# Moving GpSimd's routing-weight multiply ahead of VectorE's gating in a fused attention and mixture-of-experts kernel

## The reference

```
q, k = exp(x Wq' + bq), exp(x Wk' + bk);  v = x Wv' + bv          # 16 heads of 8
attn = causal linear attention: sum_s<=t (q_t . k_s) v_s / sum_s<=t (q_t . k_s)
x1   = layernorm(x + attn Wo' + bo)
w    = routing weights of 32 experts: sigmoid scores, best 2 of 4 expert groups,
       best 8 experts in these, normalised and scaled by 2.5; 0 for the others
y    = shared(x1) + sum_e w[t, e] * down_e( silu(gate_e x1) * (up_e x1) )
out  = layernorm(x1 + y)
```

## Time and profile before

| | us |
|---|---|
| median of 3 runs (lowest to highest) | 462.87 (462.61 to 464.24) |
| profiled execution | 463.29 |
| its span, first to last instruction | 461.5 |
| PE / PEld busy | 424.0 / 324.8 |
| DVE busy | 347.4 |
| POOL busy | 282.4 |
| ACT busy | 273.3 |

### The profile page before, as it was taken

The page is one execution under the profiler, slowest core; times in us unless marked ns, Lnnn a source line. Parts: engine busy times, 40 slices in busy tenths (PEclk is TensorE's granted clock), DMA queues, the critical chain, the costliest instruction groups (busy, mean ns, idle before and its releaser), DMA issues.

```text
span 461.5 us, 10791 instructions
## 1 busy us (share of the span) xinstructions
PE 424.0 (92%) x3954; PEld 324.8 (70%) x3954; DVE 347.4 (75%) x909; ACT 273.3 (59%) x530; POOL 282.4 (61%) x208
## 2 busy tenths in 40 slices
PE   5855799999999999999999999999999999899982
PEld 3733587778867787778877787778877787578761
DVE  2678548797878968797878968796878968777652
ACT  3835334963587546963587546963587546555642
POOL 2565236864676557864677557764677557757781
PEclk9989589999999999999999999999999999999996
DMA  7400544346440823446340923446440913466500
GB/s 233 187 1 1 147 92 90 92 97 141 93 113 7 197 69 82 91 103 135 91 116 12 202 68 74 90 104 134 91 116 9 200 41 81 91 134 129 121 11 23
DMA packets 28660, 45.08 MB, mean 98 GB/s; under 512 B 1984, under 2 KB 10304, under 8 KB 28224
## 3 DMA queue, kind: packets, MB, share of 16 engines
q1 hardware_dynamic: 28608, 44.40, 41.2%
HBM read 41.77 MB, written 2.62 MB: 96 GB/s over the span
## 4 chain that ended last, share of the span: by engine, by line
PE 40%; DVE 32%; issue 12%; POOL 8%; ACT 2%; DVEq 1%; ACTq 0%; POOLq 0%
PE bank L326 39%; DVE units L866 7%; POOL units L958 5%; DVE stats L741 2%; DVE hidden_lo L721 2%; POOL rstd L977 2%; DVE top_of_group L782 2%; DVE x L753 2%; DVE bank L775 1%; ACT hidden_hi L584 1%; DVE replaced L814 1%; DVE out_sb L878 1%; DVE k_sum L847 1%; DVE probs L731 1%; DVE kv_blocks L836 1%
## 5 line engine op out<-in xcount | busy, mean ns | idle before, releaser
L958 POOL TENSOR_TENSOR units<-units,weight_wide 128x512 f32<-128x512 f32 x128 | 174.3, 1367 | 130.5 <-DVE units L866 115.9
L602 ACT ACTIVATE units<-bank 128x512 f32<-128x512 f32 x136 | 80.7, 594 | 79.2 <-PE bank L326 78.9
L866 DVE TENSOR_TENSOR units<-bank,units 128x512 f32<-128x512 f32 x136 | 92.9, 683 | 35.1 <-PE bank L326 28.0
L584 ACT ACTIVATE hidden_hi<-units 128x512 fp32r<-128x512 f32 x136 | 86.1, 634 | 53.7 <-POOL units L958 47.7
L721 DVE TENSOR_TENSOR hidden_lo<-units,hidden_hi 128x512 fp32r<-128x512 f32 x112 | 97.7, 873 | 19.6 <-ACT hidden_hi L584 18.8
L326 PE MATMUL bank<-x_hi,gate_hi 128*128 128x512 f32 x136 | 62.1, 457 | 2.0 <-DVE units L866 1.6
L326 PE MATMUL bank<-hidden_hi,down_hi 128*128 128x512 f32 x136 | 55.0, 404 | 1.7 <-DVE hidden_lo L721 1.7
L326 PE MATMUL bank<-x_hi,up_hi 128*128 128x512 f32 x136 | 54.7, 403 | 1.8 <-ACT units L602 1.8
L326 PE MATMUL bank<-x_lo,gate_hi 128*128 128x512 f32 x136 | 54.6, 401 | 0.0
L326 PE MATMUL bank<-x_hi,gate_lo 128*128 128x512 f32 x136 | 54.4, 400 | 0.0
L326 PE MATMUL bank<-x_hi,up_lo 128*128 128x512 f32 x136 | 54.1, 398 | 0.0
(11 more groups left out here) (107 smaller groups left out, 670.8 us busy)
## 6 DMA issues: line engine op xcount, KB each, us to landing
weight_wide<-weight_d SPq DMA_DIRECT2D x62, 512.0 KB, 6.7
xT<-xT_in SPq DMA_DIRECT2D x8, 256.0 KB, 6.8
x_tok<-x_in SPq DMA_DIRECT2D x8, 256.0 KB, 6.9
out_dram<-out_sb SPq DMA_DIRECT2D x8, 256.0 KB, 2.3
weight_wide<-up_in SPq DMA_DIRECT2D x1, 1088.0 KB, 9.0
up_raw<-up_in SPq DMA_DIRECT2D x1, 1088.0 KB, 11.0
down_raw<-down_in SPq DMA_DIRECT2D x1, 1088.0 KB, 13.2
weight_d<-weightT SPq DMA_DIRECT2D x8, 64.0 KB, 1.6
```

The source lines that it names most:

```text
L584: nc.scalar.activation(hidden_hi[place(n, g)][:, :], units[place(n, g)][:, :], ACT.Copy).then_inc(hidden_hi_done, 1)
L602: nc.scalar.activation(units[place(n, g)][:, :], up_banks[2 * n % 3][:, :], ACT.Silu).then_inc(silu_done, 1)
L866: V.tensor_tensor(units[place(n, g)][:, :], up_banks[(2 * n + 1) % 3][:, :], units[place(n, g)][:, :], ALU.mult).then_inc(gated_done, 1)
L958: G.tensor_tensor(units[place(n, g)][:, :], units[place(n, g)][:, :], weight_wide[:, (n - 1) % (2 * PIECE), :], ALU.mult).then_inc(hidden_ ...
```

## The change

In groups 1 to 7 steps 3 and 4 change places for the routed blocks: POOL multiplies the silu's result by the weight as soon as the silu is done, and DVE's gating takes that product. The high part then waits for the gating. Block 0, which has no weight, and the whole of group 0 keep their order. No instruction is added or taken away, and none changes its place in its own queue; only what three of them wait for is another.

```
 high_part (ACT)
-                if n == 0:
-                    act.wait_ge(gated_done, reached(BLOCKS * g + 1))
+                if n == 0 or g > 0:
+                    act.wait_ge(gated_done, reached(BLOCKS * g + n + 1))
                 else:
-                    act.wait_ge(hidden_done, reached(ROUTED * g + n))
+                    act.wait_ge(hidden_done, n)
 slot (DVE), ahead of the gating
                     dve.wait_ge(u_ready, reached(BLOCKS * g + n + 1))
-                    dve.wait_ge(silu_done, reached(BLOCKS * g + n + 1))
+                    if g == 0 or n == 0:
+                        dve.wait_ge(silu_done, reached(BLOCKS * g + n + 1))
+                    else:
+                        dve.wait_ge(hidden_done, ROUTED * g + n)
 slot (POOL), ahead of the multiply
-                    pool.wait_ge(gated_done, reached(BLOCKS * g + n + 1))
+                    if g == 0:
+                        pool.wait_ge(gated_done, n + 1)
+                    else:
+                        pool.wait_ge(silu_done, BLOCKS * g + n + 1)
```

## The result

| | us |
|---|---|
| before, median of 4 runs (lowest to highest) | 463.21 (462.61 to 464.24) |
| after, median of 4 runs | 503.29 (501.93 to 505.33) |
| ratio, with its 95% interval | 1.087 (1.085 to 1.090) |
| profiled execution after, and its span | 502.46, 500.7 |

The changed kernel is 40.1 us slower; 497 was forecast, from 480 to 510. The lines of the changed kernel are a little lower in the file: the gating is L869, the multiply L964, the powers L973 and L983, attnT L893, x_lo L988, k_sum L950.

The account below looks back on a forecast made before the run. PE was taken to set the pace, busy 51.15 of a steady group's 51.7 us. Groups 1 to 5 add 27.5, group 6 5.0, group 7 2.0, together 34.5, giving 497 us, range 480 to 510.

Parts of the forecast that it names:

- First stall: Multiply 5 stands behind rstd2 on POOL, so gating 5 and attnT are late; PE's projection weight load slips 2.77 us.
- Second stall: Multiply 7 stands behind rstd1 on POOL, so gating 7 and block 9's gate matmul are late; +5.05 us in all.
- Given back and lost again: Later slots: router's exponential slips only 4.3 us (-0.75); then multiply 10 behind x_lo and 16 behind k_sum; +5.5 per group.
- Low parts: DVE's low part 4 is held up beside a POOL multiply, 1.57 us against a mean of 0.87.
- the walk: Step-by-step forecast through group 3 using the rows' own durations, giving +5.5 us per steady group.
- rival 2: Low parts meet running POOL multiplies more often on DVE's tight stretch: 4 us a group, 24 in all, 521; chance 0.09.
- Sum: Groups 1 to 5 add 27.5 us, group 6 5.0, group 7 2.0, group 0 nothing: 34.5 in all.
- only the first stall stays: The shorter chain behind the gating and freed DVE waits absorb all but the projection stall: +19, 482 us; chance 0.12.
- faster: Multiply hides between silu and up matmuls in slots 8 to 16 and the end: 457 us; chance 0.05.
- no effect: The gating is late only where PE has cover: 463 us; chance 0.04.
- port collisions: Some six low parts a group held 0.70 us beside POOL's multiply, on top of the forecast: 521 us; chance 0.09.
- Rival 1: Only the projection stall stays; the shorter chain behind the gating absorbs the rest: 482 us; chance 0.12.

Follow-up runs that it names:

- experiment 2: Kernel before, with gating and multiply changing places only in blocks 5 and 7 of groups 1 to 7; 487.22 us, ratio 1.051.
- experiment 5: Changed kernel with POOL's rstd2 and shift2 moved behind the multiply of block 6 and rstd1 behind that of block 7; 481.50 us, ratio 1.040.
- experiment 4: Changed kernel with rstd2 behind multiply 5, rstd1 behind multiply 7, x_lo behind multiply 10, POOL's low parts one slot later; 485.90 us, ratio 1.048.
- kernel 6: As experiment 5, but in groups 1 to 6 only blocks 1 to 9 have gating and multiply exchanged; 474.28 us, ratio 1.024.
- experiment 1: Changed kernel with POOL's rstd2 moved behind the multiply of block 5 and rstd1 behind that of block 7; 486.52 us, ratio 1.049.
- experiment 7: Changed kernel with no rstd or shift on POOL: power left out, DVE writes variance plus eps and makes shift2; 470.88 us, ratio 1.019.
- experiment 8: Kernel before with no rstd or shift on POOL: power left out, DVE writes variance plus eps and makes shift2; 454.20 us, ratio 0.981.

## Why the prediction was right

Point by point, in the order of its steps (times of after less 10.32):

- *First stall.* attnT at PE: forecast 228.10, measured 228.17; PE's wait forecast 2.77, measured 2.83. Experiments 2 and 5 confirm the cause.
- *Second stall.* The gate matmul of block 9: forecast 235.6, measured 235.27; gating 7 waited 2.21 us for POOL.
- *Given back and lost again.* The router's exponential slipped by 4.0 (forecast 4.3), gating 10 by 5.6 (5.8), gating 11 by 5.4 (5.5), gating 16 by 5.9 (5.8), the next group by 5.6 (5.5). Right in size. For gating 11 one reason was incomplete: x_lo is not what holds gating 11 back (experiment 4), the late silu with a multiply behind it is, which the prediction named as well.
- *Low parts.* Low part 4 was forecast as held and was not (0.68 us). Low parts 7 and 8 were, unforeseen (1.50 and 1.42 in the rows above). Their mean rose from 873 to 1030 ns, 17.6 us in all over 112, without moving the group's time from the walk. This is the half of rival 2 that came true: more collisions, but no 24 us; kernels 2 and 6 above show that the loss does not follow the low parts.
- *Sum.* Groups 1 to 5: forecast 27.5, measured 29.3. Group 6: 5.0 and 6.7. Group 7: 2.0 and 4.4. Group 0: 0 and -1.4. In group 7 the terms came out unlike their sizes: the late weights of block 1 cost 0.2 by block 6 (forecast 1.0), rstd2 3.2 (2.75), the silus gave back 0.8 (1.2), blocks 11 to 16, with POOL's seven instructions, lost 1.3 (1.0; the forecast's own 7 x 1.29 against 4 x 2.1 is only 0.6), and the end gave back 1.1 (1.5). The clock, below, took 1.6.

Most of the distance from 497 to 503 is TensorE's clock, of which the walk had nothing. In groups 1, 4, 6 and 7 the granted clock stood at the lower level, 1.2 GHz, for 3.4 us from 124.8, 295.5, 411.6 and 462.8; before, it did so nowhere between the start and the tail. Each of these four follows on a stall that the change made. Two stretches of 6 us, around the projection in group 6 and in group 3:

```profile
410.50:416.50 6.00, 4.63 (x18) 4.09 (x19) 4.80 (x15) 1.92 (x4) 1.34 (x3) 0.72 0.12 23
236.50:242.50 6.00, 4.00 (x21) 3.45 (x22) 5.08 (x15) 2.51 (x5) 2.25 (x4) 1.00 0.21 39
```

PE's weight loads stood still for 2.82 us in the one and 2.83 in the other, and in group 6 the clock went down 0.3 us before they began again:

```profile
411.87 1.78 PEld L326 LDWEIGHTS bank<-attn_w,attnT 128*128 128x128 f32 x8 [2.82 <-DVE attnT L893]
...
415.24 0.19 PEld L326 LDWEIGHTS bank<-x_hi,up_lo 128*128 128x128 f32 x1
```

From the attnT load to block 7's up_lo it took 3.37 us there; in group 3 it took 1.95 (238.49 to 240.44). That is +1.4 us, of which the second stall took up 0.5: block 9's gate matmul came 0.9 later in its group than in group 3. In group 7 gate, up and down of a slot took 3.73 us instead of the next slot's 2.11 (+1.6):

```profile
462.79 0.80 PE L326 MATMUL bank<-x_hi,gate_hi 128*128 128x512 f32 x1 [3.00 <-DVE units L869]
...
466.52 0.40 PE L326 MATMUL bank<-x_hi,gate_hi 128*128 128x512 f32 x1
...
468.63 0.39 PE L326 MATMUL bank<-x_hi,gate_hi 128*128 128x512 f32 x1
```

Group 4 is 1.0 above the mean of groups 1, 2, 3 and 5 (6.7 against 5.65), and group 1 lost nothing, since its second stall absorbed it. Together the clock makes some 3.5 of the 4.7 us by which the span grew beyond the forecast (39.2 against 34.5). The other 1.2 is a sum of small terms: 0.8 in groups 1 to 5 together, 0.8 in group 6, 0.8 in group 7, -1.4 in group 0 and 0.2 ahead of it. Why the same stall lowers the clock in one group and not in the next was not tried.

The rivals: *only the first stall stays* fell with the 2.17 us that PE waits ahead of block 9; *faster* with multiplies 5 and 7 running straight behind rstd; *no effect* with attnT; *port collisions* with 503 against 521 and with kernels 2 and 6. Rival 1 had held that the shorter chain behind the gating would give the time back. It freed 15.7 us of DVE's waits; PE's waits for silus and low parts fell by 4.0.

## What to carry to other kernels

Before a step is exchanged between engines, ask who waits for it afterwards and what stands ahead of it in its queue. Behind the gating the multiply had four slots until PE's `down` used its result; in front of the gating it has two until PE's gate matmuls wait for the bank, shared with three small instructions that wait for the very engine that now waits for it. POOL's four multiplies, two powers and the shift of slots 5 to 8 take 8.0 us (four of 1.25 to 1.27, 1.46, 1.33 and 0.20), in slots that lasted 9.4 us before; at 55% busy over the run the engine was nearly full where it counted.

Fix a queue's order for the whole ring of waits, not for one edge: moving the powers saved 21.8 us in one order of the gating and cost 19.4 in the other.

## What the runs showed of the hardware

- A small DVE instruction with one input was held beside a POOL multiply: the variance (128x4) took 0.82 us instead of 0.17 in experiment 1, and ended within 0.05 us of multiply 5. The Trainium skill (SBUF — State Buffer, "Who interferes with whom") says that a VectorE instruction with two SBUF inputs contends with a GpSimd one that reads SBUF, which agrees with the low parts (1.50 us beside a multiply and 1.42 beside x_lo and a multiply, 0.68 alone), and that `tensor_scalar` can enter a two-port mode in which it contends too. No run here shows in which mode the variance ran.
- A POOL power of 128x4 elements takes 1.0 to 1.6 us over all kernels, about as long as a multiply of 128x512 (1.26 to 1.30 undisturbed).
- The granted clock in the start was not the same in all kernels. Experiments 7 and 8 share group 0's order of gating and multiply with the kernel before and were some 6.5 us shorter there. The stretch of 34.5 to 64.5 us, before and then in experiment 8:

```profile
34.50:64.50 30.00, 21.77 (x322) 16.32 (x322) 18.91 (x62) 11.86 (x25) 10.15 (x6) 0.72 0.39 91
```

```profile
34.50:64.50 30.00, 25.10 (x360) 19.43 (x359) 20.57 (x56) 14.77 (x31) 12.07 (x7) 0.91 0.40 92
```

  The clock was 0.72 of full speed in the one and 0.91 in the other. How much of the 6.5 us is the clock and how much the norm without the power was not separated.
